# Graph attention with layer norm: two score tiles of each batch by ScalarE and GpSimd, x added by a DMA, statistics later

## What is computed

```
h    = x @ W[head]                      # 512 x 32 a head
th   = tanh(h)
attn = th @ w_src + (th @ w_dst)^T      # 512 x 512 a head
attn = where(attn >= 0, attn, 0.2*attn)
attn = softmax(where(adj, attn, -999))
f    = elu(attn @ h + b)                # heads side by side, 384 columns
gate = sigmoid(x @ H_w^T + H_b)
out  = layernorm(x + gate*f + (1-gate)*x)
```

## Time and profile before

| | us |
|---|---|
| median of the runs | 658.76 (658.52 to 658.85) |
| profiled execution, its own time | 658.69 |
| span of the profiled execution | 656.9 |
| mean granted TensorE clock | 0.993 of 2.4 GHz |

### The profile page before, as it was taken

How to read it: one execution, slowest core, us unless ns; L and a number is a source line. 1 busy time by engine, 2 the same in 40 slices (tenths; PEclk the granted TensorE clock), 3 DMA queues, 4 the chain that set the end, 5 groups by cost and what they waited for, 6 DMA issues and landing times.

```text
span 656.9 us, 12491 instructions
## 1 busy us (share of the span) xinstructions
PE 630.9 (96%) x3279; PEld 373.0 (57%) x3279; DVE 639.0 (97%) x1174; ACT 429.6 (65%) x936; POOL 571.4 (87%) x448
## 2 busy tenths in 40 slices
PE   8999999999999999999999999999999999999983
PEld 5565656574565647556664665656456565745531
DVE  7999999999999999999999999999999999999996
ACT  5434658486784848768485775848578584866664
POOL 2576998989989998998989999898999989997293
PEclk9999999999999999999999999999999999999997
DMA  6356549578475856848586584857747585675602
GB/s 209 118 131 181 178 123 274 128 196 248 140 235 129 235 164 176 240 146 251 133 210 190 154 238 144 249 132 200 228 142 233 139 259 126 187 211 131 217 40 97
DMA packets 54747, 117.62 MB, mean 179 GB/s; under 512 B 7106, under 2 KB 32452, under 8 KB 54724
## 3 DMA queue, kind: packets, MB, share of 16 engines
q1 hardware_dynamic: 42196, 81.56, 38.5%
q0 software_dynamic: 4320, 23.59, 19.2%
q10 hardware_dynamic: 8208, 12.19, 4.9%
HBM read 104.35 MB, written 12.98 MB: 179 GB/s over the span
## 4 chain that ended last, share of the span: by engine, by line
PE 48%; DVE 30%; issue 8%; POOL 7%; DMA 2%; ACT 2%; DVEq 1%; SPq 0%; POOLq 0%; ACTq 0%
PE out_T L1082 30%; DVE ew L820 20%; PE hg L982 13%; POOL th_w L296 4%; DVE sd L782 4%; DVE ex L842 3%; PE tr L1090 2%; POOL th_w L302 2%; PE hg L1047 1%; ACT th L471 1%; DMA xT_in<-in_xT 1%; DVE att L834 1%; DVEq L819 1%; PE hg L1014 1%; PE hg L1018 1%
## 5 line engine op out<-in xcount | busy, mean ns | idle before, releaser
L820 DVE SCALAR_TENSOR_TENSOR ew<-v_all,u,adj 128x512 f32<-128x512 f32 x768 | 522.7, 727 | 1.9 <-DMA v_all<-v_rows 1.2
L1082 PE MATMUL out_T<-ew,vals 128*64 128x512 f32 x1536 | 346.9, 597 | 0.0
L1082 PEld LDWEIGHTS out_T<-ew,vals 128*64 128x64 f32 x1536 | 106.3, 136 | 188.8 <-issue 144.1
L525 ACT ACTIVATE att_T<-out_T,out_bias 128x512 f32<-128x512 f32 x96 | 65.9, 686 | 116.1 <-PE out_T L1082 115.6
L296 POOL TENSOR_TENSOR th_w<-th,score_w 128x768 f32<-128x768 f32 x60 | 110.6, 1844 | 24.3 <-ACT th L471 24.3
L982 PE MATMUL hg<-w_hi,xT_hi 128*128 128x384 f32 x384 | 96.9, 360 | 0.8 <-ACT xT_hi L463 0.8
L982 PE MATMUL hg<-w_lo,xT_hi 128*128 128x384 f32 x384 | 88.2, 337 | 0.0
L982 PE MATMUL hg<-w_hi,xT_lo 128*128 128x384 f32 x384 | 87.7, 336 | 0.0
L302 POOL TENSOR_TENSOR th_w<-th_w 128x384 f32<-128x384 f32 x60 | 82.6, 1376 | 4.7
L982 PEld LDWEIGHTS hg<-w_hi,xT_hi 128*128 128x128 f32 x384 | 62.6, 189 | 40.2 <-issue 39.4
L982 PEld LDWEIGHTS hg<-w_lo,xT_hi 128*128 128x128 f32 x384 | 69.1, 188 | 0.0
(11 more groups left out here) (116 smaller groups left out, 669.0 us busy)
## 6 DMA issues: line engine op xcount, KB each, us to landing
v_all<-v_rows SPq DMA_DIRECT2D x95, 512.0 KB, 4.6
xT_in<-in_xT SPq DMA_DIRECT2D x16, 768.0 KB, 9.5
h_sb<-in_bias POOLq DMA_DIRECT2D x15, 768.0 KB, 6.7
x_in<-in_x SPq DMA_DIRECT2D x15, 768.0 KB, 4.6
gate_tanh<-in_H_b POOLq DMA_DIRECT2D x15, 768.0 KB, 9.4
out<-y ACTq DMA_DIRECT2D x15, 768.0 KB, 3.7
adj_in<-in_adjT SPq DMA_DIRECT2D x16, 256.0 KB, 9.8
v_rows<-v_turn SPq DMA_DIRECT2D x64, 6.0 KB
```

What stands on the lines that cost most here:

```text
L525: a.activation(att_T[:, j % 2], OUT[j % 2][:], ACT.Identity, bias=out_bias[:, q, j:j + 1]).then_inc(S["outT_copied"], 1)
L820: ve.scalar_tensor_tensor(out=twos(ew[:, (2 * C * j + i) % SLOTS, :]), in0=twos(v_all[:, j % VSLOTS, k]), scalar=u[:, q, c, h:h + 1], in1= ...
L1082: te.matmul(OUT[j % 2][VW * k:VW * k + VW, :], vals[:, q, c, h, :], ew[:, t % SLOTS, :], start=(c == 0), stop=(c == C - 1)).then_inc(S["ew ...
```

## The change

Tiles 46 and 47 of each batch (the last chunk, C - 1, of heads 10 and 11; `SIDE` = 2, and `EW` = 46 are left) are no longer made by VectorE. ScalarE computes `relu(v - u) + u` in two instructions a tile, after two small ones that negate u, and GpSimd multiplies both tiles in one instruction by `adj_side`, a bf16 copy of the last chunk's adjacency in SBUF that ScalarE makes once a batch. TensorE waits for `side_ready` ahead of tile 46. The tiles use slots 14 and 15 of the ring.

In `mix`, GpSimd writes gate times difference into y, and a DMA from its queue adds x out of DRAM onto y; `row_sums` waits for its landing. SyncE's load of `x_in` no longer waits for the mixture. `row_sums` is placed behind `out_biases`, `row_squares` in one piece behind the first two adjacency copies, `mean` behind `split_low`. Variance and scale of b-1 are no longer at the end of step b but in step b+1, between the first and the second `weigh`, and the whole `normalise` stands behind the tanh of chunk 3.

```diff
 # VectorE, edges
+                    if 2 * C * j + i >= EW:
+                        continue
 # TensorE, attend
-                        pe.wait_ge(S["ew_ready"], 4 * H * b + t + 1)
+                        if t < EW:
+                            pe.wait_ge(S["ew_ready"], EW * b + t + 1)
+                        elif t == EW:
+                            pe.wait_ge(S["side_ready"], b + 1)
 # ScalarE
+            def side_tiles(b, q):
+                act.wait_ge(S["side_ready"], b)
+                for i in range(SIDE):
+                    h = H - SIDE + i
+                    a.activation(minus_u[:, i:i + 1], u[:, q, C - 1, h:h + 1], ACT.Copy, scale=-1.0).then_inc(S["side_u"], 1)
+                act.wait_ge(ld_v[2], 32 * b + 32)
+                act.wait_ge(S["ew_free"], 4 * H * b + 4 * H)
+                act.wait_ge(S["side_u"], SIDE * b + SIDE)
+                for i in range(SIDE):
+                    k = 2 - SIDE + i
+                    a.activation(ew[:, SLOTS - SIDE + i, :], v_all[:, 2, k], ACT.Relu, bias=minus_u[:, i:i + 1]).then_inc(S["side_scored"], 1)
+                for i in range(SIDE):
+                    h = H - SIDE + i
+                    act.wait_ge(S["side_scored"], 2 * SIDE * b + i + 1)
+                    a.activation(ew[:, SLOTS - SIDE + i, :], ew[:, SLOTS - SIDE + i, :], ACT.Identity,
+                                 bias=u[:, q, C - 1, h:h + 1]).then_inc(S["side_scored"], 1)
+            def adjacency_side(b):
+                if not isinstance(b, int) or b:
+                    act.wait_ge(S["side_ready"], b)
+                a.activation(adj_side[:], adj_in[:, C - 1], ACT.Copy).then_inc(S["adj_side_done"], 1)
             def row_sums(b):
-                act.wait_ge(S["mixed"], 3 * b + 6)
+                act.wait_ge(S["add_x_done"], 16 * b + 16)
 # ScalarE, step
                 features(b + 1, 0)
-                if not isinstance(b, int) or b > 1:
-                    normalise(b - 2, 0, 2)
                 features(b + 1, 1)
                 elu_exp(b - 1, 1 - q)
                 features(b + 1, 2)
                 features(b + 1, 3)
                 if not isinstance(b, int) or b > 1:
-                    normalise(b - 2, 2, C)
+                    normalise(b - 2)
...
                 gates(b, 2)
-                row_sums(b - 1)
+                side_tiles(b, q)
                 gates(b, 3)
                 if ahead:
                     for c in range(C):
                         split(b + 2, q, c)
                 out_biases(b + 1, 1 - q)
-                row_squares(b - 1, 0, 2)
+                row_sums(b - 1)
+                copy_out(b, q, 4)
                 for c in range(2):
                     adjacency(b + 1, c)
-                copy_out(b, q, 4)
-                row_squares(b - 1, 2, C)
+                row_squares(b - 1)
+                adjacency_side(b + 1)
                 for c in range(2, C):
                     adjacency(b + 1, c)
                 copy_out(b, q, 5)
 # GpSimd
+            def side_tiles(b):
+                pool.wait_ge(S["adj_side_done"], b + 1)
+                pool.wait_ge(S["side_scored"], 2 * SIDE * b + 2 * SIDE)
+                tiles = ew[:, SLOTS - SIDE:SLOTS, :]
+                g.tensor_tensor(tiles, tiles, adj_side[:].unsqueeze(1).broadcast_to([P, SIDE, N]), ALU.mult).then_inc(S["side_ready"], 1)
             def mix(b):
                 pool.wait_ge(S["gate1_done"], b + 1)
-                pool.wait_ge(S["mixed"], 3 * b + 4)
-                g.tensor_tensor(ex[:], gate[:], ex[:], ALU.mult).then_inc(S["mixed"], 1)
-                pool.wait_ge(S["mixed"], 3 * b + 5)
+                pool.wait_ge(S["mixed"], 2 * b + 3)
                 pool.wait_ge(S["st_y"], 16 * b + 16)
-                g.tensor_tensor(y[:], x_in[:], ex[:], ALU.add).then_inc(S["mixed"], 1)
+                g.tensor_tensor(y[:], gate[:], ex[:], ALU.mult).then_inc(S["mixed"], 1)
+                pool.wait_ge(S["mixed"], 2 * b + 4)
+                pool.dma_start(y[:], x_v[b], accum_op=ALU.add).then_inc(S["add_x_done"], 16)
 # GpSimd, step
-                    for c in range(C):
+                    weigh(b + 1, 0)
+                    if not isinstance(b, int) or b > 1:
+                        variance(b - 2)
+                        scale(b - 2)
+                    for c in range(1, C):
                         weigh(b + 1, c)
...
                     values(b + 1, 1 - q)
-                if not first:
-                    mean(b - 1)
+                side_tiles(b)
                 if ahead:
                     for c in range(C):
                         if c == 0:
...
                     pool.wait_ge(S["gate_done"], C * b + C)
+                if not first:
+                    mean(b - 1)
                 add_gate_bias(b)
-                if not first:
-                    variance(b - 1)
-                    scale(b - 1)
```

More of the change, by code:

```diff
@@ L46, in gat_layernorm @@
     VB = 32
+    SIDE = 2
+    EW = 4 * H - SIDE
     assert N == 512 and H * E == D and B % 2 == 0
@@ L65, in gat_layernorm @@
         adj_in = sb("adj_in", [P, C, N], U8)
+        adj_side = sb("adj_side", [P, N], BF16)
         w_hi = sb("w_hi", [P, KD, 2 * D], F32R)
@@ L101, in gat_layernorm @@
         u = sb("u", [P, 2, C, H])
+        minus_u = sb("minus_u", [P, SIDE])
         vals = sb("vals", [P, 2, C, H, VW])
@@ L149, in gat_layernorm @@
             pool_setup dve_setup adj_done gate_bias_split gate_bias_done
-            w_hi_done w_lo_done xhi_done xlo_done h_done th_done thw_done thh_done sd_done hcopy_done g_done gate_done add_gate_bias tanh_done add_bias_done hb_sum_done hm_done
+            w_hi_done w_lo_done xhi_done xlo_done h_done th_done thw_done thh_done sd_done hcopy_done g_done gate_done add_gate_bias tanh_done add_bias_done add_x_done hb_sum_done hm_done
             scores mxT_done mxb_done exps_done v_turned vals_done
-            ew_ready ew_free outT_copied tr_done inv_done att_done
+            ew_ready ew_free adj_side_done side_u side_scored side_ready outT_copied tr_done inv_done att_done
             out_bias_done x_forms_done gate1_done elu_exp_done elu_done mixed moments sums_done mean_done squares_done var_done rstd_done y_done ld_x_last rest_last_done exp_last_done elu_last_done y_early_done elu_late_done y_late_done stats_done last_y_done""".split()
@@ L239, in step @@
                 for j in range(VSLOTS, HP):
-                    sp.wait_ge(S["ew_ready"], 4 * H * b + 2 * C * (j - 2))
+                    sp.wait_ge(S["ew_ready"], EW * b + 2 * C * (j - 2))
                     load_v(b, q, j)
@@ L246, in step @@
                     sp.wait_ge(S["x_forms_done"], b)
-                    sp.wait_ge(S["mixed"], 3 * b + 3)
                 sp.dma_start(x_in[:], x_v[b]).then_inc(S["ld_x"], 16)
@@ L253, in step @@
                         if j:
-                            sp.wait_ge(S["ew_ready"], 4 * H * b + 2 * C * (j + 4))
+                            sp.wait_ge(S["ew_ready"], EW * b + min(2 * C * (j + 4), EW))
+                        if j == VSLOTS - 1:
+                            sp.wait_ge(S["side_scored"], 2 * SIDE * b + 2 * SIDE)
                         load_v(b + 1, 1 - q, j)
@@ L270, in before @@
             def before():
-                g.sem_inc(S["mixed"], 3)
+                g.sem_inc(S["mixed"], 2)
                 g.memset(gate_bias_in, 0.0).then_inc(S["pool_setup"], 1)
@@ L442, in before @@
                     adjacency(0, c)
+                adjacency_side(0)
                 act.wait_ge(S["dve_setup"], DVE_SETUP)
@@ L503, in adjacency @@
                 if not isinstance(b, int) or b:
-                    act.wait_ge(S["ew_ready"], 4 * H * b - 2 * C + 4 * (c // 2) + 4)
+                    act.wait_ge(S["ew_ready"], EW * b + (0 if c // 2 else SIDE - C))
                 a.activation(ADJ_WORDS[c // 2][:, c % 2], adj_in[:, c].bitcast(U16), ACT.Copy).then_inc(S["adj_done"], 1)
+            def adjacency_side(b):
+                if not isinstance(b, int) or b:
+                    act.wait_ge(S["side_ready"], b)
+                a.activation(adj_side[:], adj_in[:, C - 1], ACT.Copy).then_inc(S["adj_side_done"], 1)
             def out_biases(b, q):
@@ L528, in x_forms @@
                 act.wait_ge(S["ld_x"], 16 * b + 16)
-                act.wait_ge(S["mixed"], 3 * b + 3)
+                act.wait_ge(S["mixed"], 2 * b + 1)
                 a.activation(x_plus1[:], x_in[:], ACT.Identity, bias=plus1[:, 0:1]).then_inc(S["x_forms_done"], 1)
@@ L545, in gate_quarter_pass @@
                     act.wait_ge(S["tanh_done"], b + 1)
-                act.wait_ge(S["mixed"], 3 * b + 2)
+                act.wait_ge(S["mixed"], 2 * b + 2)
                 a.activation(gate[:], gate_tanh[:], ACT.Identity, bias=quarter[:, 0:1], scale=0.25).then_inc(S["gate1_done"], 1)
@@ L669, in x_last_form @@
                 act.wait_ge(S["ld_x_last"], 16)
-                act.wait_ge(S["mixed"], 3 * (B - 1) + 1)
+                act.wait_ge(S["mixed"], 2 * (B - 1) + 1)
```

(2 more changed lines are left out.)

## The result

| | before | after |
|---|---|---|
| median of the runs, us | 658.73 (658.52 to 658.85) | 713.27 (713.21 to 713.29) |
| ratio after to before | | 1.083, 95% interval 1.081 to 1.085 |
| span of the profiled execution, us | 656.9 | 711.5 |
| mean granted TensorE clock | 0.993 | 0.988 |

The account below looks back on a forecast made before the run. A ring of waits across four engines was taken to set the 38.85 us batch. It grows 2.0 + 1.1 = 3.1 us, 13 times: 40.3; with -1.3 and +2.5, 658.7 + 41.5 = 700.2 us; 8-in-10 range 670 to 722.

Parts of the forecast that it names:

- The ring: Chain of waits from M to M over TensorE, ScalarE, GpSimd, VectorE; sets the 38.85 us batch, grows by 3.1 us.
- The two tiles that VectorE lost: Tiles 46 and 47, made while TensorE carries the ring: 1.3 us a batch becomes a longer wait for chunk 0, worth 0.
- The stage of ScalarE: Gates 2 to tanh: side tiles add 1.6 us, waiting for the mean 0.6; tanh at M + 23.4, +2.0 us a batch.
- M: Start of the transpose of the maxima on TensorE, once a batch; 354.86 in the batch analysed, next at 393.58.
- The variance: GpSimd, between chunks 0 and 1: 2.1 us make chunk 1 late; VectorE waits +1.1 us a batch (0.9 to 2.1).
- The adding DMA: Replaces 3.47 us of GpSimd; lands 6.7 to 10.2 us after issue, just hidden before ScalarE asks at M + 15.5.
- The first batches: At the start the chain runs along VectorE's tiles, so two tiles fewer gain 1.3 us once.
- The last batch: Early columns of y come at about 648, behind DMA landing, side tiles and GpSimd's product: +2.5 us, 0 to 5.
- Rival 1: VectorE, 97% busy, was the bound and the change relieves it: 651 us; chance 0.08.
- the rule that the prediction names beside it: Trainium skill: take the engine with highest occupancy; when VectorE is saturated, moving work to ScalarE or even GpSimd may pay.
- Rival 2: Only the variance counts: ScalarE's additions cost under 1.6 us or start earlier, tanh stays put; 674 us, chance 0.13.
- Rival 3: DMA lands after 12 us or GpSimd's product costs 3.5: 1.1 to 2 us more; 715 to 726, chance 0.14.

Follow-up runs that it names:

- the last experiment: Kernel before with the maxima of the scores taken one tile earlier on VectorE, before tile 7 of pair 2 instead of tile 8: 657.39 us, ratio 0.9972.
- the short batch above: One of eight 41.1 to 41.8 us loop batches in the changed kernel with the elu one tile earlier on VectorE; that run measured 713.47 us.

## Why the prediction was right, and where it was off

*The bound.* Right. The ring was the bound: its pieces account for 45.4 of the 54.5 us, and the last experiment shows that little lay under it. The two tiles that VectorE lost were worth nothing, as forecast: they became a wait for adjacency (2.66 and 0.92 us) instead of the wait for chunk 0 that I had named; VectorE reaches head sum 0 at the same moment as chunk 0 gets ready.

*The stage of ScalarE.* Right within 0.2 us: tanh at M + 23.28 against M + 23.4. Inside it two errors partly cancel: the instructions were dearer (side tiles 2.79 us and bf16 copy 0.52, 3.3 together against 3.2) and the wait for the mean shorter, since GpSimd's product took 2.14 us instead of 2.4: 0.17 us of visible wait against 0.6.

*The variance.* The place was right and the size in the range (1.55 against 1.1, 0.9 to 2.1), but the step "with 2.1 us more it is ready at 386.4, and VectorE waits 1.1 us" failed as a mechanism. I took it that only GpSimd loses while the elu runs. Whoever comes second loses: here first the elu, by 1.56 us, then GpSimd's halving add, as before. VectorE's head sum did not wait for GpSimd: chunk 1 was ready at 412.19 (409.79 + 2.40), 1.03 us ahead of its head sum, as in the kernel before. Without the elu's 1.56 us the head sum would have waited some 0.5 us for it; this is an estimate from these rows. The nearest measured case is the short batch above, with 0.33. So it is partly luck that 1.1 came near 1.55: the wait that I priced was at most half there, and the loss came from an instruction that I had at its old length. The difference is 0.45 us a batch, 5.9 in all.

*The adding DMA.* Right in the loop: landed within 7.2 to 7.8 us, no wait, and without it the kernel is 11 us slower.

*The order of sums and squares.* I had it at nothing apart from the wait for the mean. Without side tiles it is not nothing: some 0.3 us a batch on the tanh. In the changed kernel the side tiles fill the idle stretch that it leaves.

*The first batches.* Wrong: the 1.3 us did not come, and no row that I showed carried them. M of step 1 is at 82.95 before and at 82.92 after.

*The last batch.* Under-sized: 2.5, 0 to 5, against 9.1. The step "I get the early columns at about 648" counted only the landing of the adding DMA and the side tiles. It overlooked that the product, which now writes y itself, also takes over the addition's wait for the store of y (3.42 us), and that the gate's bias DMA is late (1.73 us): issued behind the mean, at M + 16.7 instead of M + 14.2, it took 11.2 us to land, more than any of that line before (10.2). It also had no collision on VectorE near the end (1.87 us instead of 0.69). Side tiles alone make the tail 2.2 us longer, order and DMA 4.1, against 9.2 in all; how the rest comes about is not settled. TensorE's clock may have a part in it: behind a wait of 3.70 us at 664.65 it was 0.82 over 7.9 us, and before, behind 1.59 us, 1.00.

*The rivals.* Rival 1, and with it the rule that the prediction names beside it, is refuted for this kernel by the side tiles alone (681.4, not 651). Rival 2 fell with M + 23.28. Rival 3 fell by its range, 715 to 726, though by only 1.7 us, and by its mechanism: the DMA landed in at most 7.8 us, and the product took 2.14. The result lies at the upper edge of the forecast's own range, 681 to 714.

*The sum.* I forecast 41.5 us and 54.5 came. Of the 13.0 between them the last batch has 6.6 (9.1 - 2.5), the first batches 1.3, and the loop 5.1 (45.4 - 40.3): 5.9 for the elu (13 x 0.45) and 1.2 for the head sum behind the tanh (13 x 0.09), less 2.0 for ScalarE's stage (13 x 0.15).

## What to carry to other kernels

Read the spare time of an engine in the stage where the new work will be issued, not in its share of the span: ScalarE was 65% busy and had 1.65 us to spare where 3.3 were put. When two engines are nearly full, look for the ring that sets the period, and ask of each moved instruction whether it lies on it; work taken from an engine elsewhere only lengthens its waits. And when something small is moved on GpSimd, see which of its long instructions then begins just ahead of a VectorE instruction with two inputs in SBUF.

## What the runs showed of the hardware

An elementwise VectorE instruction with two SBUF inputs (the elu, 128x1536) and a GpSimd tensor_tensor hold each other up, and the later one pays: the elu took 3.31 us when GpSimd had begun 0.13 us earlier, and GpSimd's instruction took 2.54 instead of 1.03, or 1.48 instead of 0.20, when the elu had begun 0.07 or 0.34 us earlier. What it pays is nearly what the other still has to run: 1.56 of 1.69 us, 1.51 of 1.68 and 1.28 of 1.42 in these three cases. The tiles, whose second input is in PSUM, took 0.68 to 0.75 us in every run. The Trainium skill (SBUF — State Buffer, Who interferes with whom, and Summary: rules for kernel authors) says that a VectorE instruction with two SBUF inputs contends with a GpSimd instruction that reads SBUF, and that the second to issue is blocked until the first has finished; these numbers agree.

TensorE's granted clock was 1.00 behind every gap of 1.57 to 1.80 us before the transposes of pair 5. With the elu one tile earlier the gap was 2.15 to 2.34 us in seven batches; the clock was 0.72 to 0.74 over the 6.0 us of features behind it in five of them and 1.00 in two (gaps of 2.20 and 2.21). With x added by GpSimd the gap was 2.62 to 2.85 us in all 13 batches, and the clock was 0.72 to 0.80 in eight and 1.00 in five. So the length of the gap alone doesn't tell which level follows, and in that run the batches stayed at 43.3 to 43.5 us either way.
